# Routed rows gathered into the accumulators, tokens added to the shared expert's outputs, and the second pair's raw weights issued earlier

## The reference

```python
xn = layernorm(x)
# attention: latents of width 128, 16 heads, causal, scores clipped to +-80
c_Q, c_KV = xn @ W_DQ.T, xn @ W_DKV.T
scores = q_C @ k_C.T + rope(q_R) @ rope(k_R).T
out = softmax(clip(scores) / sqrt(192)) @ v @ W_O.T
# experts: 3 of 7 by a softmax gate, shares normalised to sum 1
y = ffn(xn, Ws1, Wsg, Ws2)
for e in range(7):
    y = y + ffn(xn, W1[e], Wg[e], W2[e]) * w_e     # ffn: silu(x@w1) * (x@wg) @ w2
return x + out + y
```

## Time and profile before

| | us |
|---|---|
| median of 3 runs | 1333.8 (1333.33 to 1334.8) |
| profiled execution | 1334.99 |
| its span, first to last instruction | 1333.0 |
| PE busy | 1304.3 (98%) |
| PE weight loads busy | 1090.8 (82%) |
| DVE busy | 736.7 (55%) |
| POOL busy | 627.9 (47%) |
| ACT busy | 620.4 (47%) |

### The profile page before, as it was taken

The page is one execution under the profiler, slowest core; times in us unless marked ns, Lnnn a source line. Parts: engine busy times, 40 slices in busy tenths (PEclk is TensorE's granted clock), DMA queues, the critical chain, the costliest instruction groups (busy, mean ns, idle before and its releaser), DMA issues.

```text
span 1333.0 us, 21124 instructions
## 1 busy us (share of the span) xinstructions
PE 1304.3 (98%) x6553; PEld 1090.8 (82%) x6553; DVE 736.7 (55%) x1349; ACT 620.4 (47%) x1146; POOL 627.9 (47%) x534
## 2 busy tenths in 40 slices
PE   5999999999999999999997999999999999999999
PEld 4788888888888888888885888888888888888887
DVE  6361154332222222222224878988888888788876
ACT  6421243222222222222224766676667666766674
POOL 5125584994060005000003467666766676666543
PEclk9999999999999999999998999999999999999999
DMA  8225453664142114212115123233233332322012
GB/s 268 65 87 220 185 187 96 186 187 143 57 151 64 57 57 127 86 57 64 57 52 181 34 47 70 65 64 74 39 83 63 61 64 58 77 43 60 17 48 95
DMA packets 72952, 123.23 MB, mean 92 GB/s; under 512 B 10960, under 2 KB 19280, under 8 KB 72848
## 3 DMA queue, kind: packets, MB, share of 16 engines
q1 hardware_dynamic: 42000, 60.49, 15.8%
q0 software_dynamic: 11312, 27.23, 9.5%
q10 hardware_dynamic: 19536, 34.17, 7.7%
HBM read 74.41 MB, written 39.05 MB: 85 GB/s over the span
## 4 chain that ended last, share of the span: by engine, by line
PE 94%; DVE 2%; DMA 1%; SPq 1%; POOL 1%; issue 1%; ACT 0%; ACTq 0%; DVEq 0%; POOLq 0%
PE bank L48 83%; PE bank L1676 4%; PE bank L1461 2%; PE bank L1403 2%; PE bank L1546 1%; SPq L442 1%; DMA rows_b<-in_x 1%; DMA raw<-in_wot 0%; PE bank L1389 0%; POOL slots L484 0%; DVE stats L905 0%; DVE store_b L1291 0%; SPq L428 0%; PE bank L1522 0%; DVE acc L1318 0%
## 5 line engine op out<-in xcount | busy, mean ns | idle before, releaser
L48 PE MATMUL bank<-store_b,store_a 128*128 128x512 f32 (+1 forms) x1536 | 322.8, 363 | 2.2 <-DVE store_b L1217 1.9
L48 PE MATMUL bank<-slots,x_turned 128*128 x1296 | 317.6, 394 | 0.3 <-DVE x_turned L929 0.3
L48 PEld LDWEIGHTS bank<-store_b,store_a 128*128 128x128 f32 x1536 | 255.4, 190 | 54.1 <-issue 9.0
L48 PEld LDWEIGHTS bank<-slots,x_turned 128*128 128x128 f32 x1296 | 239.3, 188 | 48.1 <-issue 0.5
L951 DVE TENSOR_TENSOR hid_t<-bank,hid_t 128x512 fp32r<-128x512 f32 x70 | 48.3, 691 | 343.6 <-ACT hid_t L668 343.6
L48 PE MATMUL bank<-slots,hid_t 128*128 (+1 forms) x840 | 208.4, 397 | 0.0
L48 PE MATMUL bank<-store_b 128*128 128x512 f32 x768 | 179.4, 389 | 0.0
L48 PEld LDWEIGHTS bank<-slots,hid_t 128*128 128x128 f32 x840 | 153.7, 188 | 31.1 <-DVE hid_t L951 0.3
L48 PEld LDWEIGHTS bank<-store_b 128*128 128x128 f32 x768 | 144.1, 188 | 29.9
L842 ACT ACTIVATE p_store<-bank 128x512 f32<-128x512 f32 x160 | 95.6, 597 | 86.2 <-PE bank L48 84.6
L538 POOL CAST slots<-staging 128x512 f32 (+1 forms) x84 | 51.7, 615 | 171.7 <-PE bank L48 169.5
(11 more groups left out here) (203 smaller groups left out, 1820.9 us busy)
## 6 DMA issues: line engine op xcount, KB each, us to landing
staging<-in_w SPq DMA_DIRECT2D x56, 256.0 KB, 2.8
sorted_y<-y_store ACTq DMA_DIRECT2D x54, 256.0 KB, 2.0
rows<-sorted_x ACTq DMA_DIRECT2D x51, 260.0 KB, 2.7
rot_sin<-sum_b SPq DMA_DIRECT2D x128, 64.0 KB, 2.0
staging<-in_wg SPq DMA_DIRECT2D x28, 256.0 KB, 2.8
shared_y<-y_store ACTq DMA_DIRECT2D x16, 256.0 KB, 2.4
raw<-in_wot SPq DMA_DIRECT2D x16, 256.0 KB, 2.9
acc<-in_x SPq DMA_DIRECT2D x16, 256.0 KB, 5.6
```

Of the source, the lines that this page charges most:

```text
L48: made = pe.matmul(out, a, b, start=first and n == 0, stop=last and n == len(pairs) - 1, skip_group_check=onto)
```

## The change

1. `acc` is no longer loaded with the tokens. In the shared blocks ACT issues loads of token tiles into `y_store` (`load_tokens`), and DVE adds bank 3 to them (`add_tokens`) in place of ACT's copy. ACT stores the sum to `shared_y` (`store_shared`). SP loads `acc` from `shared_y`.
2. The ring `moe`, its 16 loads and DVE's 16 additions are gone. POOL gathers the routed rows straight into `acc`, for the batch whose output was added two units before, in the same units 2 to 25, two per unit. DVE's `output` waits for the gathers of its batch.
3. SP issues the raw weights of pair 1 right after `swap_halves(0)`, ahead of the 16 loads of `acc`.

```diff
@@ sync_program
             swap_halves(0)
+            for h in heads_of(0):
+                head_weights(1, h)
             sp.wait_ge(on["y_done"], NBK)
+            for n in range(2):
+                sp.wait_ge(on[f"y_sent{n}"], 16 * (NT // 2))
             for b in range(NB):
                 for t in range(b * TB, (b + 1) * TB):
-                    sp.dma_start(acc[:, t, :], x_t[:, t, :]).then_inc(on[f"x_back{b}"], 16)
+                    sp.dma_start(acc[:, t, :], shared_y[t]).then_inc(on[f"shared_back{b}"], 16)
...
-                    sp.dma_start(moe[:, t % NM, :], shared_y[t]).then_inc(on[f"base_in{t % NM}"], 16)
...
-                for h in heads_of(u):
+                for h in heads_of(u) if u else ():
                     head_weights(p + 1, h)
@@ pool_program, end of unit u
-                n, j = divmod(u - 2, TOP_K)
-                if 0 <= n < NT // 2:
-                    gather(2 * n, j)
-                    gather(2 * n + 1, j)
+                if u >= 2 and u - 2 < NT // 2 * TOP_K:
+                    n, b = divmod(u - 2, NB)
+                    pool.wait_ge(on["out_added"], TB * (u - 1))
+                    if n:
+                        pool.wait_ge(on[f"part_in{b}"], 32 * n)
+                    gather(b * TB + n // TOP_K * 2, n % TOP_K)
+                    gather(b * TB + n // TOP_K * 2 + 1, n % TOP_K)
@@ scalar_program
+            def load_tokens(b):
+                if b >= 2:
+                    act.wait_ge(on[f"y_sent{b % 2}"], 16 * (b // 2))
+                act.dma_start(y_store[:, b % 2, :], x_t[:, b, :]).then_inc(on[f"token_in{b % 2}"], 16)
+            def store_shared(b):
+                act.wait_ge(on["y_evicted"], b + 1)
+                act.dma_start(shared_y[b], y_store[:, b % 2, :]).then_inc(on[f"y_sent{b % 2}"], 16)
...
                 turn(1)
-                evict(NT - 1)
+                store_shared(NT - 1)
...
+                if 2 <= b < NT:
+                    store_shared(b - 2)
+                    if b > 2:
+                        load_tokens(b - 1)
+                if b >= NT + 2:
                     evict(b - 2)
                 silu(b)
@@ vector_program
+            def add_tokens(b):
+                dve.wait_ge(on["y_done"], b + 1)
+                dve.wait_ge(on[f"token_in{b % 2}"], 16 * (b // 2 + 1))
+                dve.tensor_tensor(y_store[:, b % 2, :], banks[3], y_store[:, b % 2, :], ALU.add).then_inc(
+                    on["y_evicted"], 1)
...
                 for t in range(1, NT):
                     project(t)
                     turn(t - 1)
+                    if t == 2:
+                        add_tokens(NT - 1)
...
+                if 2 <= b < NT:
+                    add_tokens(b - 2)
...
-                for t in (2 * n, 2 * n + 1) if u % 3 == 2 and 0 <= n < NT // 2 else ():
...
-                    dve.tensor_tensor(acc[:, t, :], moe[:, t % NM, :], acc[:, t, :], ALU.add).then_inc(
-                        on["moe_added"], 1)
```

More of the change, by code:

```diff
@@ L241, in program @@
         rot_raw = sum_b[:].rearrange("p h t -> p (h t)")
-        NM = 5
-        moe = tile(ctx, "moe", [P, NM, D], side="right")
         sems(*(f"x_in{n}" for n in range(NT)), "scattered0", "scattered1", "padded0", "padded1", *(f"staged{n}" for n in range(NS)), *(f"row_in{n}" for n in range(3)),
              *(f"y_sent{n}" for n in range(2)), "gate_in", "consts_in", "zeros_in",
-             "cat_in", *(f"x_back{b}" for b in range(NB)), *(f"base_in{n}" for n in range(NM)), *(f"part_in{n}" for n in range(NM)),
+             "cat_in", *(f"shared_back{b}" for b in range(NB)), "token_in0", "token_in1", *(f"part_in{b}" for b in range(NB)),
              "rope_in", "angles_in", "raw_in0", "raw_in1", "wr_in",
@@ L573, in gather @@
             def gather(t, j):
[L575 to L580, removed]
+                pool.indirect_dma_start(acc[:, t, :], None, sorted_y,
                                         bass.IndirectOffsetOnAxis(ap=place[:, t, j:j + 1], axis=0),
-                                        compute_op=ALU.add).then_inc(on[f"part_in{s}"], 16)
+                                        compute_op=ALU.add).then_inc(on[f"part_in{t // TB}"], 16)
             sine(0)
@@ L789, in scalar_program @@
                     projections()
-                if b >= 2 and b not in (NT, NT + 1):
+                if b == 1:
+                    load_tokens(0)
+                    load_tokens(1)
+                if 2 <= b < NT:
[3 more added lines that the diff above has]
+                if b >= NT + 2:
                     evict(b - 2)
@@ L1312, in output @@
                 if p == 0 and tt == 0:
-                    dve.wait_ge(on[f"x_back{b}"], 16 * TB)
-                if tt == 0 and u >= 5:
-                    dve.wait_ge(on["moe_added"], min(2 * ((u - 2) // 3), NT))
+                    dve.wait_ge(on[f"shared_back{b}"], 16 * TB)
+                if p and tt == 0:
+                    dve.wait_ge(on[f"part_in{b}"], 32 * min(p, TB // 2 * TOP_K))
                 if p:
```

24 lines of the change are left out of this document (9 added, 15 removed).

## The result

The changed kernel takes 1336.9 us (median of 9 runs, 1334.4 to 1338.2), the kernel before beside it 1333.6 (9 runs, 1333.1 to 1334.8): ratio 1.0021, 95% interval 1.0012 to 1.003. So the change makes this kernel slower, by about 0.2%, 2 to 3 us.

A forecast was written before the change was run, and what follows sets the result against it. PE was taken as the bound, busy 1304.3 of 1333.0 us. The terms 1.0 - 1.55 - 0.7 + 0.8 = -0.45 (a loss) put the median at 1333.8 + 0.45 = 1334.2 us, with an 8-in-10 range of 1331.0 to 1337.2.

The forecast's parts named there:

- The gap of 6.57 us: Unit 0, PE's wait for raw: about 8.6 us hang on it, but removing it gains PE only 1.85.
- None of it waits for PE's head weights, so it stays where it is: Unit 0 to 1: the chain swap, POOL sine, sums, rotate, ACT, DVE keeps its time, ending at 735.89.
- If instead it is the 4 MB of `acc` ahead of it, nothing moves. I take the second: Last swap in unit 0: held by acc's loads ahead, gain 1.85 us; if by raw loads behind, 3.95.
- The clock: Around unit 0's two new waits, PE falling to 1.2 GHz was put at 0.45 us lost, at worst 1.6.
- The follow-up in unit 1: Unit 1: DVE comes late out of unit 0, rotate_low(2) has 0.14 to spare, so PE loses some 0.4 us.
- part 3's sum: Start of attention, raw weights sooner: 1.85 - 0.4 - 0.45 = 1.0 us gained, bounds -0.15 and 3.95.
- Part 1, shared blocks: Blocks 4 to 7: ACT's silu behind DVE's addition makes PE wait, 1.55 us lost, bounds 0 and 4.
- Rival 2: Blocks 4 to 7: the gate's chain through DVE, ACT and DVE loses 5.5 us, time 1338.2; chance 0.15.
- Projections: Near turn(3): the addition behind turn(1) delays kr for project(3), 0.7 us lost, bounds 0.3 and 1.3.
- Part 2: Units 12, 23 and 24: 16 additions leave DVE, 0.8 us gained, bounds 0 and 1.3.
- a whole iteration to land: Shared blocks: token loads, 4 MB more DMA over 130 us, have 8.6 us each to land.
- slower: Whole kernel slower by over 0.2%, above 1336.5 us: chance 0.17.

The follow-up runs named there:

- e4: Changed kernel with swap_halves(1) issued ahead of the sixteen loads of acc: 1332.9 us, ratio to before 0.9987.
- e1: Kernel before with only the earlier raw weights of pair 1 (behind swap_halves(0)) added: 1334.6 us, ratio to before 1.0002.
- e3: Changed kernel with ACT's store and token load behind silu and hid_high in blocks 4 to 7, last shared block stored later: 1334.1 us, ratio to before 1.0004.
- e11: Changed kernel loading only 8 of 512 token columns for blocks 2 to 15 (small tokens): 1336.7 us, ratio to before 1.002.
- e5: Changed kernel with the edits of e3 and e4 together: 1329.4 us, ratio to before 0.9962.
- e8: e5 with DVE's order changed at the start of attention (rotate_low(0) and queries earlier, unit 1's queries later): 1327.0 us, ratio to before 0.9938.

## Why the prediction came out as it did

- **The gap of 6.57 us is worth little: right.** The two waits that were to take its place are there by engine and line, and the raw wait is gone. Their sizes are 5.05 and 1.23 us (2.53 and 1.23 in the second profile) against 3.4 and about 3.
- **"None of it waits for PE's head weights, so it stays where it is": right, shown by e4.** The chain hangs on the swaps: with them ahead of `acc`, 4.6 to 5.6 us of column C come back.
- **"If instead it is the 4 MB of `acc` ahead of it, nothing moves. I take the second": half wrong.** The 4 MB are the large part (`sine(1)` 6.9 us sooner in e4). But with the raws gone from behind the swaps it also starts sooner, by 0.5 us in the first profile and by 1.3 in the mean of six profiles against four. From the last swap's issue to `sine(1)` it is 6.8 us with them behind (6.4 to 7.1, four profiles) and 6.1 without (5.8 to 6.5, six). I had said that I am wrong if this is over 1 us; in four of the six it was. The Trainium skill ("DMA: Bandwidth & Descriptors", Queues, rings and completion order) has descriptors of one queue taken in ring order on each DMA engine. By that alone the raws behind could do nothing. The 1.3 don't bear that out, and 0.9 of them are already there when the last load of `acc` lands (16.0 us behind the first one's issue in the four, 15.1 in the six), so it isn't the swaps alone that come sooner. What makes the difference was not tried.
- **The clock: mis-sized.** I put 0.45 us on it, hoping that the low stretch might fall into the waits. The clock was low behind the last wait in all five profiles with part 3 alone or in the change (after twice, e1, e3, e11), which cost 1.7 to 2.2 us, 2.05 in the mean. With the earlier swaps the two errors cancel: 1.85 + 1.3 - 2.05 = 1.1, and the forecast's 1.0 stands against 1.1 in column C. The follow-up in unit 1 that I costed at 0.4 shows no wait. So part 3's sum was right by luck, two errors against each other, and in the times part 3 is worth 0 within 1.2 us.
- **Part 1, shared blocks: right, slightly low.** Forecast 1.55, measured 1.7 in after and 1.8 in the mean of six profiles. Place by place, from PE's starts: `down(3)` 0.44 later (forecast 0.55), one block on 0.14 (0), `down(5)` 0.73 (0.8), then 0.29 and 0.13 (0.2). e3 shows the cause: only ACT's place in the chain was changed, and all of it came back. Rival 2 had this mechanism with waits of 3.95 us in all, and 1.6 more for the clock, which stayed at full here.
- **Projections: too low.** Forecast 0.7 (0.3 to 1.3). In B the six profiles with the early addition average 0.8 and the five without it -0.3, so 1.1; two profiles of before differ by 0.6. I had reckoned with "some is regained" of 1.0; none was. In after PE waits 0.67 us at 190.19, where I had one wait of 1.0 near 189, and 0.70 more at 197.34, again for ACT's `store_a`, which I had not forecast. Such a wait of 0.7 is in all versions with part 1 but e3, and moves with the edits (to 205.42 in e5 and 206.08 in e8, where the addition comes later); what makes it stays open.
- **Part 2: too high.** Forecast 0.8, measured 0.5 in column D, at units 23 and 24 as forecast (0.65 there); of the 0.25 at unit 12 only 0.1 shows in after. The new waits cost nothing, as said.
- **What I had missed:** the loads of tokens against the scatter. I had written that they have "a whole iteration to land", and looked only at what waits for them, not at what shares the DMA engines with them.
- **The sum:** 1.1 - 1.8 - 1.1 + 0.5 = -1.3, against -0.45 forecast and 2 to 3.2 us in the medians. The terms that were off are the projections by 0.4, part 2 by 0.3 and the shared blocks by 0.25, all to the slow side. Some 1 us of the measured loss has no place in the stretches, with an interval of 1.2 us on each ratio; I leave it open. The sign was right, and the mistake was to put 0.17 on "slower" with a sum that was already negative and terms that were bounded unevenly to the slow side.

## What to carry to other kernels

When a wait goes, ask what its transfer's neighbours in the same queue were holding: here the loads that nobody needed for 40 us stood ahead of 256 KB that four engines needed, and putting them behind it gave back 4.6 to 5.6 us of PE's path and 3.4 to 4.0 of the median. An operation moved from one engine to another takes its new engine's queue with it: an addition that costs 0.68 us and has slack of its own held ACT's table load for `silu` by 2 us, because DVE did the gate first. And count transfers as load on what shares the DMA engines, even where nobody waits for them.

## What the hardware showed that I had not expected

- Short waits were enough for half clock in unit 0. In e4 the clock was still at 1.00 for over 2 us behind a wait of 0.71 us and fell ahead of the one of 0.19 (windows of e4, columns as in the earlier trace rows); the ten scores took 4.98 us instead of 2.56.

```profile
727.20:729.40 2.20, 2.20 (x17) 2.07 (x17) 0.00 (x0) 0.39 (x1) 1.77 (x2) 1.00 1.04 381
729.60:736.20 6.60, 6.41 (x18) 4.81 (x18) 5.14 (x11) 4.55 (x11) 0.00 (x0) 0.50 0.57 214
```

- The fall is not the same in each execution. The first scores, behind the same 1.9 us wait, took 4.12, 3.66, 2.52 and 4.11 us in the two profiles of before and the two of after.
- DVE and POOL hold each other up in unit 0 when the swaps are early. DVE's subtraction of two SBUF operands took 0.68 us alone and 1.75 beside POOL's `sine(1)`, and POOL's 1.26 us operations took 1.64 and 1.74 (rows of e4 above and below). The Trainium skill ("SBUF — State Buffer", SBUF: two separate sides) says that the two engines share a port pair, which an instruction of DVE with two SBUF inputs and one of POOL that reads SBUF can't hold together: the one that starts first keeps it to its end. The trace agrees: the slow subtraction starts 0.44 us behind POOL's `sine(1)` and ends 0.6 us behind its end, which is about the 0.68 that it takes alone.

```profile
721.91 1.75 DVE L1307 TENSOR_TENSOR store_b<-p_store,store_b 128x512 fp32r<-128x512 f32 x1
```

- 3.5 MB of plain loads over 100 us stretched POOL's chain of over 50 scatters by some 10 us, though the DMA engines were busy only 0.61 of the time from 90 to 190 us (0.56 in before and with small tokens).
